# A graph and attention kernel: the edges' keys and degrees formed on GpSimd instead of VectorE

## The chip, the cores and the metric

The kernel runs on one core of one Trainium2 chip. The metric is device time in microseconds of one execution. A core has five engines that run side by side, each with a queue of its own: TensorE (PE, matrix products), VectorE (DVE), ScalarE (ACT), GpSimd (POOL) and SyncE (SP, which issues transfers). They meet through semaphores: an instruction adds to one when it is done, and another engine waits until it has reached a count.

## What is computed

The reference is a network of two layers over 3125 nodes with 256 features and 100,000 edges, sorted by destination. Each layer adds three things to x: a graph convolution over the edges, a linear attention, and a mixture of experts. What matters here is the first layer's graph part and attention, and the weights of the second layer's graph part:

```python
xn = _layernorm(x, axis=-1)
neigh = segment_sum(xn[src], dst, num_segments=n)      # layer 0, graph
h = (1.0 + eps) * xn + neigh
...
k = softmax(concat([mk, k], axis=-1), axis=-1)         # layer 0, attention
context = einsum('bhdn,bhen->bhde', k, v)
out = einsum('bhde,bhdn->bhen', context, softmax(q, axis=-2) * SCALE)
...
deg = segment_sum(ew2, dst2, num_segments=n_nodes)     # layer 1, graph
dinv = where(deg > 0, rsqrt(maximum(deg, 1e-30)), 0.0)
norm = dinv[src2] * ew2 * dinv[dst2]
```

The kernel doesn't gather rows edge by edge. It builds a dense matrix of edge counts and one of edge weights from one-hot matrices, and multiplies with them.

## The kernel before

**Edges in windows.** Destinations are cut into 1564 windows of two nodes each. Window number 128 g + p lies on partition p in group g, with 13 groups (`WG`) and so 13 x 128 = 1664 (`WN`) edge places on each partition. GpSimd's `windows_pool` gathers for every window 128 edges that start near its first one, 13 gathers of (dst, src, weight) triples into `H`. The views `edst`, `esrc` and `eew` are the three columns of these triples, so each steps over three words; `wrel` and `wlo` are written over `edst` and `esrc`.

**What VectorE does with them.** `places_dve` (13 instructions, `L323`) turns each destination into its place in the window: 0.5 or -0.5 in `wrel` for an edge of this window, anything else for a stranger. ScalarE squares that (`places_act`, `L334`), and `inside_dve` (`L338`) tests the square against 0.25 and counts the edges inside. `places_in_tiles_dve` splits the sender into a tile of 128 nodes (`L341`, a shift) and a place in it (`L343`, `wlo`). `tiles_dve` (`L347`) and `keys_dve` (`L351`) form the key from tile, place and test. TensorE turns `wlo` and the keys (`places_pe`, `keys_pe`), and ScalarE (`keys_act`) and VectorE (`keys16_dve`, `L404`) write them as bf16. `weights_dve` (`L310`, 26 instructions of 128 columns, each with a sum) forms the degree that each window gives to its two nodes, and signals `fold` 26 times; `degrees_pool` scales and stores it. `total_pe` and `good_dve` add the counts over the partitions and compare the sum with 100,000: where it differs, a slow path takes over.

**Attention around it.** `mix0_dve`, `mix0_act` and `mix0_pe` hold the order of work of this stage, written out by hand, and the edges' steps are set between those of the attention. In the loop over the seven groups j of tiles, TensorE turns the queries into a bank, ScalarE copies them to one of two buffers `qt`, TensorE multiplies with the context (`outs_pe`, `L816`), ScalarE takes squares and a root, and VectorE scales and adds to X (`L949` to `L959`). `keys_pe` stands behind the outputs of group 0 in TensorE's order. The buffers `qt` are the first two of the four 512-wide parts of `SC`:

```python
    qt = [SC[:, i, :] for i in range(2)]
    junk = [yob[0][:, 0, :], yob[0][:, 1, :], yob[1][:, 1, :], SC[:, 2, 0:D]]
```

**Behind it.** `count_pe`, `count_act` and `count_dve` run over 391 octets of windows in 25 blocks: VectorE makes one-hot matrices (`L1014` to `L1019`), TensorE multiplies them (`L1040` to `L1045`), and ScalarE brings the results out (`L1061`).

Of the kernel before, what the change touches and what calls it, by code (L numbers as in the profile page):

```python
# [20 lines left out]
EDGES = 100000  # L21
# [50 lines left out]
def program(nc, ctx, a, out):  # L72
# [96 lines left out]
    wprod = [wide_wb[:, i:i + 128] for i in range(2944, 2944 + 2 * WN, 128)]  # L169
# [3 lines left out]
    inside, goodc = pick[:, 65:66], pick[:, 66:67]  # L173
    deg2 = small[:, 970:970 + 2 * WG].rearrange("p (g r) -> p g r", r=2)
# [111 lines left out]
    def begins_dve(e, c):  # L286
        e.wait_ge(S("drow"), 16 * WG)
        for g in range(WG):
            c.add(e.tensor_scalar(rowf[:, g, :], rowi[:, g, :], w2h[:, g:g + 1], None, ALU.is_lt, ALU.add, accum_out=beg4[:, g:g + 1]))
        c.wait()  # L290
        c.add(e.scalar_tensor_tensor(beg4, row4, 128.0, beg4, ALU.mult, ALU.add))
        c.wait()
        e.tensor_copy(beg4i, beg4).then_inc(S("begins"), 1)

    def windows_pool(e):
        e.wait_ge(S("rows"), 1)
        for g in range(WG):
            e.indirect_dma_start(rowi[:, g, :], None, a["dst"].rearrange("(r k) -> r k", k=128),
                                 bass.IndirectOffsetOnAxis(ap=row4i[:, g:g + 1], axis=0)).then_inc(S("drow"), 16)
        e.wait_ge(S("begins"), 1)  # L300
# [6 lines left out]
    def weights_dve(e):  # L307
        for g in range(WG):
            for r in range(2):
                e.scalar_tensor_tensor(wprod[2 * g + r], wrel[:, g, :], r - 0.5, eew[:, g, :], ALU.is_equal, ALU.mult,  # L310
                                       accum_out=deg2[:, g, r:r + 1]).then_inc(S("fold"), 1)

    def degrees_pool(e):
        e.wait_ge(S("fold"), 2 * WG)
# [7 lines left out]
    def place_dve(e, g):  # L322
        return e.tensor_scalar(wrel[:, g, :], edst[:, g, :], w2h[:, g:g + 1], 1.0, ALU.subtract, ALU.subtract)  # L323

    def places_dve(e, c):
        e.wait_ge(S("edges"), 16 * WG)
        for g in range(WG - 1):
            c.add(place_dve(e, g))
        c.wait()
        place_dve(e, WG - 1).then_inc(S("mix0_dve"), 1)  # L330

    def places_act(e):
        e.wait_ge(S("mix0_dve"), M0V_REL + 1)
        e.activation(wok, wrel, ACT.Square).then_inc(S("mix0_act"), 1)  # L334

    def inside_dve(e):
        e.wait_ge(S("mix0_act"), M0A_PLACES + 1)
        e.tensor_scalar(wok, wok, 0.25, None, ALU.is_le, ALU.add, accum_out=inside).then_inc(S("inside"), 1)  # L338

    def places_in_tiles_dve(e, c):  # L340
        c.add(e.tensor_scalar(whii.bitcast(I32), esrc, 7, None, ALU.logical_shift_right))  # L341
        c.wait()
        e.scalar_tensor_tensor(wlo, whii.bitcast(I32), -128.0, esrc, ALU.mult, ALU.add).then_inc(S("wkey"), 1)  # L343

    def tiles_dve(e, c):
        e.wait_ge(S("wkey"), 1)
        c.add(e.scalar_tensor_tensor(whii, whii.bitcast(I32), 2.0, wrel, ALU.mult, ALU.add))  # L347

    def keys_dve(e, c):
        c.wait()  # L350
        e.scalar_tensor_tensor(wkey, whii, 1.5, wok, ALU.add, ALU.mult).then_inc(S("wkey"), 1)  # L351
# [22 lines left out]
    def places_pe(e):  # L374
        e.wait_ge(S("wkey"), 1)
# [3 lines left out]
    def keys_pe(e):  # L379
        e.wait_ge(S("wkey"), 2)  # L380
# [9 lines left out]
    def good_dve(e):  # L390
        e.wait_ge(S("total"), 1)
        e.tensor_scalar(goodc, B[3][:, 0:1], float(EDGES), None, ALU.is_equal).then_inc(S("good"), 1)
        e.tensor_scalar(flagi[0:1, 0:1], B[3][0:1, 0:1], float(EDGES), None, ALU.is_equal).then_inc(S("good"), 1)
# [261 lines left out]
    M0V_W, M0V_RS, M0V_GROW, M0V_REL, M0V_KMAX, M0V_DIAG, M0V_KSUB, M0V_MEM, M0V_MASKED, M0V_CTX, M0V_CWO = (  # L655
# [173 lines left out]
    def mix0_act(e):  # L829
# [71 lines left out]
    def mix0_dve(e, c):  # L901
        places_dve(e, c)
# [23 lines left out]
        inside_dve(e)  # L926
        q_norm_dve(e, c, 0)
        places_in_tiles_dve(e, c)
        good_dve(e)
# [14 lines left out]
        weights_dve(e)  # L944
# [259 lines left out]
    def count_act(e):  # L1204
        highs_act(e, 2)
        for b in range(T + 6):
            for i in range(8):
                if has_batch(b, i):
                    hots_act(e, 8 * b + i)
                if b == 0 and 1 <= i < 6:  # L1210
                    if i == 1:
                        e.wait_ge(S("fold"), 2 * WG)
# [113 lines left out]
    def degrees_dve(e, i, c):  # L1326
        if i == 4:
# [3 lines left out]
            e.tensor_scalar(dcol, dcol, 1.0, 1e-30, ALU.add, ALU.max).then_inc(S("degmax"), 1)  # L1331
        if i == 6:
            e.wait_ge(S("degroot"), 1)
# [4 lines left out]
    def degrees_act(e, i):  # L1338
        if i == 5:
            e.wait_ge(S("degmax"), 1)  # L1340
# [1362 lines left out]
```

## Time and profile before

| what | us |
|---|---|
| median of 3 runs (2229.63 to 2230.86) | 2230.41 |
| span of the profiled execution, first to last instruction | 2231.0 |
| its own time beside the span | not shown apart from it; the span lies 0.6 above the median of the runs |
| busy: PE 2089.4, DVE 1653.8, ACT 1233.5, POOL 566.9 | of 2231.0 |

A busy time says how long an engine was at work in all; it doesn't say in which stretch it held the others up. For that one reads the busy times of each stretch, and ahead of an instruction the idle time of its engine with what ended it.

### The profile page before, as it was taken

What the parts mean: (1) busy time and instruction counts of PE and PEld (TensorE: products, weight loads), DVE (VectorE), ACT (ScalarE), POOL (GpSimd) and SP (SyncE); (2) the same over time, 40 slices, a digit from 0 to 9 for tenths busy, and PEclk for the clock granted to TensorE, in tenths of its full rate; (3) what the DMA queues carried; (4) which work ended last, traced back from release to release, by engine and by line L of the source; (5) the groups of instructions that cost most, each with busy time, mean ns of one, the idle gap of its engine ahead of it and who ended that gap; (6) DMA issues with size and microseconds to landing.
All of it is one profiled execution on the core that took longest, in us unless ns stands there. A gap on an engine that the chain in (4) does not pass through costs nothing. (4 is left out here: it accounts for less than half of the span.)

```text
span 2231.0 us, 47270 instructions
## 1 busy us (share of the span) xinstructions
PE 2089.4 (94%) x18287; PEld 1958.7 (88%) x18287; DVE 1653.8 (74%) x3108; ACT 1233.5 (55%) x2876; POOL 566.9 (25%) x406
## 2 busy tenths in 40 slices
PE   5659999999879999998999999999999999999997
PEld 3549999999779999997788999999988999999996
DVE  6899888886578888884667666565667768888885
ACT  5656555555537677674543444444444336767664
POOL 3100000000036777761000000000000015777775
PEclk9879999999989999998999999999999999999998
DMA  4424343333448778775003666466641026777776
GB/s 123 145 65 115 96 114 90 99 111 104 161 158 234 236 218 241 227 222 144 1 26 89 189 188 182 122 182 195 189 145 47 25 93 184 239 231 222 240 215 171
DMA packets 241114, 339.04 MB, mean 152 GB/s; under 512 B 33407, under 2 KB 202546, under 8 KB 240754
## 3 DMA queue, kind: packets, MB, share of 16 engines
q1 hardware_dynamic: 208908, 296.19, 42.4%
q0 software_dynamic: 28528, 35.76, 8.6%
q10 hardware_dynamic: 3446, 3.97, 0.6%
q8 instruction: 150, 2.46, 0.5%
q14 instruction: 82, 0.67, 0.1%
HBM read 258.89 MB, written 76.95 MB: 151 GB/s over the span
## 5 line engine op out<-in xcount | busy, mean ns | idle before, releaser
L2011 POOL DMA_INDIRECT SC<-xd,slot_i x128 | 181.6, 1419 | 1423.8 <-DVE slot_q L1647 1291.6
L2436 PE MATMUL bank<-WB_r,XN_r 128*128 128x448 f32 x1400 | 398.7, 366 | 0.4 <-DVE X L2253 0.4
L2390 DVE TENSOR_TENSOR WB_r<-WB,WB_r 128x448 fp32r<-128x448 f32 x350 | 214.8, 624 | 169.1 <-ACT WB_r L2385 169.0
L2385 ACT CAST WB_r<-WB 128x448 fp32r<-128x448 f32 x350 | 198.2, 568 | 244.8 <-PE bank L2436 242.9
L2436 PEld LDWEIGHTS bank<-WB_r,XN_r 128*128 128x128 f32 x1400 | 262.4, 188 | 23.0 <-DVE X L2253 0.8
L1941 PE MATMUL bank<-SC_r,WB_r 128*128 128x256 f32 (+1 forms) x2064 | 250.8, 280 | 8.4 <-issue 6.3
L1941 PEld LDWEIGHTS bank<-SC_r,WB_r 128*128 128x128 f32 x2064 | 244.3, 188 | 12.6 <-issue 12.4
L1061 ACT CAST WB_r<-bank 128x200 fp32r<-128x200 f32 x391 | 145.3, 372 | 164.7 <-PE bank L1045 163.9
L1956 PE MATMUL bank<-R_r,H_r 128*128 128x256 f32 x1752 | 216.6, 283 | 5.0 <-DVE R_r L1852 5.0
L1956 PEld LDWEIGHTS bank<-R_r,H_r 128*128 128x128 f32 x1752 | 210.4, 190 | 5.4 <-issue 5.4
L1804 ACT ACTIVATE wb_<-bank,WB 128x256 f32<-128x256 f32 (+1 forms) x344 | 133.3, 477 | 79.7 <-PE bank L1941 40.6
L2017 POOL DMA_INDIRECT slot_p<-pd,slot_q x128 | 160.7, 1255 | 63.5 <-issue 35.7
L1941 PE MATMUL bank<-SC_r,XN_r 128*128 128x256 f32 x1392 | 169.5, 280 | 5.5 <-issue 4.9
L1941 PEld LDWEIGHTS bank<-SC_r,XN_r 128*128 128x128 f32 x1392 | 164.8, 188 | 9.5 <-issue 9.2
L1813 ACT ACTIVATE yo<-yo,slot_p 128x256 f32<-128x256 f32 x118 | 53.7, 502 | 209.0 <-DVE yo L1891 130.0
L1101 PE MATMUL bank<-H_r,WB_r 128*128 128x256 f32 x625 | 165.1, 300 | 0.0
L2436 PE MATMUL bank<-WB_r,R_r 128*128 128x448 f32 x448 | 164.5, 367 | 0.0
L1101 PE MATMUL bank<-XN_r,WB_r 128*128 128x256 f32 x625 | 154.0, 281 | 0.0
L1061 ACT COPY X<-bank 128x200 f32<-128x200 f32 x391 | 149.9, 383 | 0.0
L1015 DVE TENSOR_TENSOR SC<-R,DR 128x1024 bf16<-128x1024 bf16 x196 | 134.0, 684 | 0.0
L1101 PEld LDWEIGHTS bank<-XN_r,WB_r 128*128 128x128 f32 x625 | 119.3, 191 | 0.1
L1101 PEld LDWEIGHTS bank<-H_r,WB_r 128*128 128x128 f32 x625 | 119.0, 190 | 0.1
(462 smaller groups left out, 5139.1 us busy)
## 6 DMA issues: line engine op xcount, KB each, us to landing
WB<-adjw SPq DMA_DIRECT2D x350, 224.0 KB, 2.8
WB<-in_f_pack SPq DMA_DIRECT2D x127, 512.0 KB
WB<-in_f_pack SPq DMA_DIRECT2D x62, 640.0 KB
adjw<-X SPq DMA_DIRECT2D x24, 1600.0 KB, 7.6
WB<-in_f_pack SPq DMA_DIRECT2D x65, 516.0 KB
xd<-XN SPq DMA_DIRECT2D x15, 640.0 KB, 5.5
y<-X SPq DMA_DIRECT2D x10, 640.0 KB, 3.3
X<-y SPq DMA_DIRECT2D x6, 640.0 KB, 7.0
```

The source lines that it names most:

```text
L1015: e.tensor_tensor(by_two(hot_lo[s][:, 0:m, :]), row(iota16, o), along(lo2, o, 128), ALU.is_equal).then_inc(S("lo1"), 1)
L1061: e.copy(to[b % 2][:, :, 8 * j:8 * j + 8].rearrange("p h (q r) -> p q h r", r=2), bank[:, :, i]).then_inc(S(name), 1)
L1101: m = e.matmul(bk[:, 0:D], CNT[b % 2][:, h, :], x[:, h * D:(h + 1) * D], start=(h == 0 and x is xnh), stop=(h == T - 1 and x is xnl), skip ...
L1804: m = e.activation(st[:, q * w:(q + 1) * w], B[hp][:, q * TS:q * TS + w], gfun[L], bias=b[:, hc:hc + 1])
L1813: e.activation(ob[:, q, :], ob[:, q, :], ACT.Copy, scale=slot_p[:, 2 * i + q:2 * i + q + 1]).then_inc(S("obs"), 1)
L1941: m = e.matmul(B[hp][:, q * TS:q * TS + w], p[:, c * HID + hc * 128:c * HID + (hc + 1) * 128], x[:, c * w:(c + 1) * w], start=(c == 0 and ...
L1956: m = e.matmul(bk[:, s * D:(s + 1) * D], x[:, hc * w + s * 128:hc * w + (s + 1) * 128], p[:, hc * D:(hc + 1) * D], start=(hc == 0 and n == ...
L2011: e.indirect_dma_start(yin[i % 2][:, q * D:(q + 1) * D], None, XD, bass.IndirectOffsetOnAxis(ap=slot_i[:, 2 * i + q:2 * i + q + 1], axis=0 ...
L2017: e.indirect_dma_start(slot_p[:, 2 * i + q:2 * i + q + 1], None, PD.rearrange("(r k) -> r k", k=1), bass.IndirectOffsetOnAxis(ap=slot_q[:, ...
L2385: e.copy(split_w(m)[0], RAW[m % PR]).then_inc(S("whigh"), 1)
L2390: e.tensor_tensor(al, RAW[m % PR], ah.bitcast(F32), ALU.subtract).then_inc(S("wlow"), 1)
L2436: mm_ = e.matmul(conv_bank(k, band, c)[:, 0:PW], x[st][:, o], y, start=(st == 0 and i == 0), stop=(st == T - 1 and i == 2))
```

## The change

VectorE keeps one instruction for the edges, the shift (`tiles_dve`, now at the place of the placements and on all 1664 columns). Everything else moves to a new program of GpSimd, `edges_pool`, which runs behind its own gathers: the 13 placements, the sender's place, the key, the test, the counts and the degrees. VectorE's sums along a row, which were a by-product of an instruction, become additions of halves: 128 columns to 64, 32 and so on to 1, for all 13 groups at once (`sum_of_rows_pool`, seven instructions). Each step on GpSimd waits for the semaphore `edge` of the step before it. The count keeps its 13 groups apart (`kept`), and VectorE adds them behind the sum over the partitions. The products of the weights move from 26 pieces of `WB` to the first 1664 columns of `SC`, where the two buffers `qt` lie; ScalarE therefore waits for `fold` ahead of its first copy to `qt`.

```diff
-    wprod = [wide_wb[:, i:i + 128] for i in range(2944, 2944 + 2 * WN, 128)]
+    wprod = sc_all[:, 0:WN].rearrange("p (g n) -> p g n", g=WG)
...
-    def weights_dve(e):
+    PLACED, SCALED, SENDER, HALVED, TILED, KEPT, INSIDE, KEYED = (
+        WG, WG + 2, WG + 3, WG + 4, WG + 5, WG + 6, WG + 13, WG + 14)
+
+    def sum_of_rows_pool(e, of, to, n):
+        src, k = of, 64
+        while k:
+            dst = to if k == 1 else wprod[:, :, 0:k]
+            e.tensor_tensor(dst, src[:, :, 0:k], src[:, :, k:2 * k], ALU.add).then_inc(S("edge"), 1)
+            n += 1
+            e.wait_ge(S("edge"), n)
+            src, k = dst, k // 2
+        return n
+
+    def edges_pool(e):
+        e.wait_ge(S("edges"), 16 * WG)
         for g in range(WG):
-            for r in range(2):
-                e.scalar_tensor_tensor(wprod[2 * g + r], wrel[:, g, :], r - 0.5, eew[:, g, :], ALU.is_equal, ALU.mult,
-                                       accum_out=deg2[:, g, r:r + 1]).then_inc(S("fold"), 1)
+            e.tensor_scalar(wrel[:, g, :], edst[:, g, :], w2h[:, g:g + 1], 1.0, ALU.subtract, ALU.subtract).then_inc(S("edge"), 1)
+        e.wait_ge(S("mix0_dve"), M0V_TILE + 1)
+        e.tensor_scalar(wlo, esrc, 1.0, None, ALU.mult).then_inc(S("edge"), 1)
+        e.tensor_scalar(wprod, whii.bitcast(I32), -128.0, None, ALU.mult).then_inc(S("edge"), 1)
+        e.wait_ge(S("edge"), SCALED)
+        e.tensor_tensor(wlo, wlo, wprod, ALU.add).then_inc(S("edge"), 1)
+        e.tensor_scalar(whii, wprod, -1.0 / 64, 1.5, ALU.mult, ALU.add).then_inc(S("edge"), 1)
+        e.wait_ge(S("edge"), HALVED)
+        e.tensor_tensor(whii, whii, wrel, ALU.add).then_inc(S("edge"), 1)
+        e.wait_ge(S("mix0_act"), M0A_PLACES + 1)
+        e.tensor_scalar(wok_flat, wok_flat, 0.25, None, ALU.is_le).then_inc(S("edge"), 1)
+        e.wait_ge(S("edge"), KEPT)
+        sum_of_rows_pool(e, wok, kept.unsqueeze(2), KEPT)
+        e.tensor_tensor(wkey_flat, whii_flat, wok_flat, ALU.mult).then_inc(S("edge"), 1)
+        n = KEYED
+        for r in range(2):
+            e.wait_ge(S("edge"), n)
+            e.tensor_scalar(wprod, wrel, r - 0.5, None, ALU.is_equal).then_inc(S("edge"), 1)
+            e.wait_ge(S("edge"), n + 1)
+            e.tensor_tensor(wprod, wprod, eew, ALU.mult).then_inc(S("edge"), 1)
+            e.wait_ge(S("edge"), n + 2)
+            n = sum_of_rows_pool(e, wprod, deg2[:, :, r:r + 1], n + 2)
+        e.sem_inc(S("fold"), 2)
...
-    def places_dve(e, c):
+    def tiles_dve(e):
         e.wait_ge(S("edges"), 16 * WG)
-        for g in range(WG - 1):
-            c.add(place_dve(e, g))
-        c.wait()
-        place_dve(e, WG - 1).then_inc(S("mix0_dve"), 1)
+        e.tensor_scalar(whii.bitcast(I32), esrc, 7, None, ALU.logical_shift_right).then_inc(S("mix0_dve"), 1)
...
     def places_pe(e):
-        e.wait_ge(S("wkey"), 1)
+        e.wait_ge(S("edge"), SENDER)
...
     def keys_pe(e):
-        e.wait_ge(S("wkey"), 2)
+        e.wait_ge(S("edge"), KEYED)
...
     def total_pe(e):
         e.wait_ge(S("set"), 4)
-        e.wait_ge(S("inside"), 1)
-        e.matmul(B[3][:, 0:1], ones[:, :], inside, start=True, stop=True).then_inc(S("total"), 1)
+        e.wait_ge(S("edge"), INSIDE)
+        e.matmul(B[3][:, 0:WG], ones[:, :], kept, start=True, stop=True).then_inc(S("total"), 1)
...
+                if j == 0:
+                    e.wait_ge(S("fold"), 2)
                 if j >= 2:
                     e.wait_ge(S("ot"), 4 * (j - 1))
                 e.copy(qt[j % 2][:, 0:n], B[j % 2][:, 0:n]).then_inc(S("qt"), 1)
...
     def pool_program(e):
         windows_pool(e)
+        edges_pool(e)
         degrees_pool(e)
```

In `mix0_dve` the calls of the removed functions go, and in the rest of the diff semaphores get other names and counts (`begins` becomes a second count of `rows`, `degmax` a first one of `degroot`).

## Rows read from the trace of the kernel before

**Rows 1.** The page's totals: span, then busy us of each engine.

```profile
span 2231.0 us, 47270 instructions
PE 2089.4 (94%) x18287; PEld 1958.7 (88%) x18287; DVE 1653.8 (74%) x3108; ACT 1233.5 (55%) x2876; POOL 566.9 (25%) x406
```

**Rows 2.** Busy us (instructions) by stretch: PE, PEld, DVE, ACT, POOL, then clock, DMA.

```profile
104.00:120.00 16.00, 9.21 (x49) 7.74 (x49) 15.79 (x66) 7.91 (x23) 0.37 (x1) 0.89 0.00 0
...
146.00:182.00 36.00, 25.06 (x449) 24.24 (x450) 35.60 (x61) 23.39 (x69) 0.00 (x0) 0.72 0.22 66
182.00:300.00 118.00, 117.79 (x2018) 112.59 (x2015) 98.53 (x188) 67.12 (x262) 0.00 (x0) 1.00 0.40 113
```

**Rows 3.** Waits, 182 to 440 us: in total, times, longest.

```profile
DVE wb_ L1014 <- PE bank L1045: 43.4, 54, 1.2
```

**Rows 4.** VectorE in order of time: start us, us, what, count.

```profile
72.09 0.31 DVE L323 TENSOR_SCALAR H<-H,CB 128x128 f32<-128x128 int32 x1
...
72.31 2.80 DVE L323 TENSOR_SCALAR H<-H,CB 128x128 f32<-128x128 int32 x12
...
89.46 1.87 DVE L338 TENSOR_SCALAR_CACHE_REDUCE R<-R 128x1664 f32<-128x1664 f32 x1
...
94.91 1.34 DVE L341 TENSOR_SCALAR wide_wb<-H 128x1664 int32<-128x1664 int32 x1
96.28 2.46 DVE L343 SCALAR_TENSOR_TENSOR H<-wide_wb,H 128x1664 f32<-128x1664 int32 x1
...
99.25 2.45 DVE L347 SCALAR_TENSOR_TENSOR wide_wb<-wide_wb,H 128x1664 f32<-128x1664 int32 x1
...
101.81 1.89 DVE L351 SCALAR_TENSOR_TENSOR R<-wide_wb,R 128x1664 f32<-128x1664 f32 x1
...
108.92 3.85 DVE L404 TENSOR_SCALAR DR<-bank,small 128x1024 bf16<-128x1024 f32 x4
112.68 0.33 DVE L310 SCALAR_TENSOR_TENSOR wide_wb<-H 128x128 f32<-128x128 f32 x1
...
119.29 0.20 DVE L949 TENSOR_SCALAR small<-small 128x4 f32<-128x4 f32 x1
```

**Rows 5.** VectorE's groups by shape, 65 to 125 us: busy us, mean ns.

```profile
L878 DVE TENSOR_TENSOR wide_wb<-wide_wb,small 128x1408 f32<-128x1408 f32 x2 | 3.2, 1624 | 0.1
...
L922 DVE TENSOR_TENSOR wide_wb<-wide_wb,small 128x1408 f32<-128x1408 f32 x2 | 3.2, 1622 | 0.0
...
L878 DVE TENSOR_TENSOR wide_r<-wide_r,small 128x384 f32<-128x384 f32 x1 | 0.6, 558 | 0.0
...
L708 DVE TENSOR_SCALAR small<-small 128x25 f32<-128x25 f32 x1 | 0.2, 167 | 0.0
```

**Rows 6.** GpSimd in order of time: its last gather and its one arithmetic instruction.

```profile
61.96 0.94 POOL L302 DMA_INDIRECT H<-in_edges,small x1 [0.30 <-issue]
119.51 0.37 POOL L316 TENSOR_SCALAR small<-small 128x26 f32<-128x26 f32 x1 [56.61 <-DVE wide_wb L310]
```

**Rows 7.** DMA, 60 to 70 us in 40 slices: busy tenths of each.

```profile
DMA  7730966309384074663000000000000000000000
```

**Rows 8.** ScalarE in order of time: the squares, the first copy, the first root.

```profile
77.88 2.44 ACT L334 ACTIVATE R<-H 128x1664 f32<-128x1664 f32 x1
...
103.12 0.58 ACT L852 COPY SC<-bank 128x512 f32<-128x512 f32 x1 [0.61 <-PE bank L797]
...
110.41 0.20 ACT L863 ACTIVATE small<-small 128x4 f32<-128x4 f32 x1
```

**Rows 9.** The line of GpSimd's degree scaling: its queue's instructions, first and last start.

```profile
L316 POOLq MODIFY_POOL_CONFIG  x2: 42/42/43, 62.9 to 62.9; - x2
```

**Rows 10.** TensorE in order of time: the total, first outputs, key transposes.

```profile
91.48 0.35 PE L388 MATMUL bank<-small,ones 128*128 128x1 f32 x2
...
104.65 3.57 PE L816 MATMUL bank<-yo,SC 128*128 128x256 f32 x8
108.06 1.58 PE L371 MATMUL bank<-CB,R 128*128 128x128 f32 x13
```

More of the change, by code:

```diff
@@ L292, in begins_dve @@
         c.wait()
-        e.tensor_copy(beg4i, beg4).then_inc(S("begins"), 1)
+        e.tensor_copy(beg4i, beg4).then_inc(S("rows"), 1)
     def windows_pool(e):
@@ L299, in windows_pool @@
                                  bass.IndirectOffsetOnAxis(ap=row4i[:, g:g + 1], axis=0)).then_inc(S("drow"), 16)
-        e.wait_ge(S("begins"), 1)
+        e.wait_ge(S("rows"), 2)
         for g in range(WG):
@@ L313, in degrees_pool @@
     def degrees_pool(e):
-        e.wait_ge(S("fold"), 2 * WG)
+        e.wait_ge(S("fold"), 2)
         e.wait_ge(S("good"), 1)
@@ L318, in degrees_pool @@
         e.dma_start(DEG.rearrange("(g p r) -> p g r", g=WG, r=2), deg2).then_inc(S("deg_out"), 16)
[L322 to L325 removed]
+    def tiles_dve(e):
         e.wait_ge(S("edges"), 16 * WG)
[L327 to L330 removed]
+        e.tensor_scalar(whii.bitcast(I32), esrc, 7, None, ALU.logical_shift_right).then_inc(S("mix0_dve"), 1)
     def places_act(e):
[L333 removed]
+        e.wait_ge(S("edge"), PLACED)
         e.activation(wok, wrel, ACT.Square).then_inc(S("mix0_act"), 1)
[L336 to L345, printed above, removed]
[L346 to L351 removed]
     FILLS = 4
@@ L386, in total_pe, with good_dve @@
         e.wait_ge(S("set"), 4)
-        e.wait_ge(S("inside"), 1)
-        e.matmul(B[3][:, 0:1], ones[:, :], inside, start=True, stop=True).then_inc(S("total"), 1)
-    def good_dve(e):
+        e.wait_ge(S("edge"), INSIDE)
+        e.matmul(B[3][:, 0:WG], ones[:, :], kept, start=True, stop=True).then_inc(S("total"), 1)
+    def good_dve(e, c):
         e.wait_ge(S("total"), 1)
-        e.tensor_scalar(goodc, B[3][:, 0:1], float(EDGES), None, ALU.is_equal).then_inc(S("good"), 1)
-        e.tensor_scalar(flagi[0:1, 0:1], B[3][0:1, 0:1], float(EDGES), None, ALU.is_equal).then_inc(S("good"), 1)
+        c.add(e.tensor_reduce(inside, B[3][:, 0:WG], AX, ALU.add))
+        c.wait()
+        e.tensor_scalar(goodc, inside, float(EDGES), None, ALU.is_equal).then_inc(S("good"), 1)
+        e.tensor_scalar(flagi[0:1, 0:1], inside[0:1, :], float(EDGES), None, ALU.is_equal).then_inc(S("good"), 1)
     def keys_act(e):
@@ L849, in mix0_act @@
                 e.wait_ge(S("qT"), j + 1)
+                if j == 0:
+                    e.wait_ge(S("fold"), 2)
                 if j >= 2:
@@ L901, in mix0_dve @@
     def mix0_dve(e, c):
-        places_dve(e, c)
+        tiles_dve(e)
         q_sub_dve(e, c, 1)
@@ L1211, in count_act @@
                     if i == 1:
-                        e.wait_ge(S("fold"), 2 * WG)
+                        e.wait_ge(S("fold"), 2)
                     e.copy(xnh[:, fifth(i - 1)], xn_all[:, fifth(i - 1)]).then_inc(S("xnh"), 1)
@@ L1330, in degrees_dve @@
             c.wait()
-            e.tensor_scalar(dcol, dcol, 1.0, 1e-30, ALU.add, ALU.max).then_inc(S("degmax"), 1)
+            e.tensor_scalar(dcol, dcol, 1.0, 1e-30, ALU.add, ALU.max).then_inc(S("degroot"), 1)
         if i == 6:
-            e.wait_ge(S("degroot"), 1)
+            e.wait_ge(S("degroot"), 2)
             c.add(e.reciprocal(dcol, dcol))
```

15 lines of the change are left out of this document (6 added, 9 removed).

## The prediction

> **What bounds the kernel now.** I read the page's totals first, then the busy time by stage, the waits of the long stage, and last the rows of each engine around the change. The totals name TensorE, 2089.4 of 2231.0 us [rows 1], but that is an average over stages with different limits. By stages [rows 2]: from 104 to 120 us VectorE works 15.79 of 16 us, from 146 to 182 it works 35.60 of 36, and TensorE about 60 to 70% in both. From 182 us TensorE works 117.79 of 118 and VectorE waits for it: 43.4 us in 54 waits up to 440 us [rows 3]. So the edges' preparation and the attention loop behind it belong to VectorE, and TensorE's long run starts when VectorE has fed it. Neither stage waits for a transfer, so whatever moves the attention loop (`L949` and below, first row at 119.29 us [rows 4]) moves the end by as much.
>
> **What comes off VectorE.** Rows 4 hold the pieces: 13 placements (0.31 and 2.80, nearly back to back, 2.9 together), the count `L338` 1.87, the remainder `L343` 2.46, the keys `L347` and `L351` 2.45 and 1.89, and 26 degree passes from 112.68 to 119.29, 6.6. That is 18.2 us. The shift `L341`, 1.34, is only moved to the place of the placements. Added is one reduction over 13 columns of a bank and its wait; the small VectorE row of [rows 5], 0.17, bounds it, and nothing bounds it at 1 us or more. If nothing else held the loop, VectorE would reach it at about 119.3 - 18.0 = 101.3 us, a gain of 18 us. This is the gain that the change is after; the question is what GpSimd costs.
>
> **What GpSimd gets.** Its gathers were issued by 62.9 us [rows 6] and the transfers had ended by about 64.8 [rows 7]: of 40 slices of 0.25 us the last busy one is the 19th. Then it was idle until 119.5. Thirteen placements fit there: at VectorE's 0.31 us they take 4 us, at 2.2 times that (below) 8.9, so they end between 69 and 74 us. ScalarE's squares need them at 77.88 [rows 8], so they are covered, and they would cost only if they took over 1 us each. Two configuration instructions stand in GpSimd's queue at 62.9 [rows 9]; whatever they start was hidden behind that idle time and now has 8.6 us of it left, so I price it at nothing, at most the few microseconds by which it passes 73.4. At 73.4 (72.09 + 1.34) VectorE's shift is ready and the serial chain of GpSimd begins. Each step waits for the one before it:
>
> - six passes over 128x1664 with one input (sender to float, tile times -128, the affine step, the test for 0.25, twice the test for the row);
> - four with two inputs, one of them strided in the edges' tile (low part, key, two products with the weights), and the key times its test, contiguous;
> - three sums by halves, seven additions each, 1651 elements.
>
> The trace shows no such pass on GpSimd, so I price it from both sides. VectorE's prices are the lower side: one input 1.34 (`L341`), strided two inputs 2.45 (`L347`), contiguous 1.89 (`L351`) [rows 4]. For the additions, the 1408- and 384-wide rows give (1624 - 558)/1024 = 1.04 ns an element and 0.16 us fixed [rows 5], so a sum costs 7 x 0.16 + 1651 x 0.00104 = 2.8. Together 6 x 1.34 + 4 x 2.45 + 1.89 + 3 x 2.83 = 28.2 us. The chain would then end at F = 73.4 + 28.2 = 101.6. The other side is GpSimd's one arithmetic row, 0.37 us for 128x26 [rows 6]. Read as a rate it is 14 ns an element, which would put F hundreds of microseconds later; read against VectorE's 0.167 us for 128x25 of the same kind of instruction, a tensor with a scalar [rows 5], it says that GpSimd takes 2.2 times as long. I take the ratio: it is the one pair of rows in which both engines do the same thing at nearly the same size, though both are mostly fixed cost. Then the chain is 28.2 x 2.22 = 62.6 us and F = 136.
>
> The Trainium skill, GPSIMD Engine Reference, section Performance versus the Vector engine, says that a GpSimd addition of two float tensors takes 1.96 times VectorE's time, while one-input work is near line rate; it also advises against moving elementwise work there. The 2.2 of the row agrees in direction. By the page's figure on the two-input passes alone the sum would be 8.0 + 1.96 x 20.2 = 47.6, F = 121 and the time about 2241.
>
> **The wait that this makes.** The products now live in the first 1664 columns of `SC`, which also holds the two `qt` buffers. So ScalarE's first copy to `qt` waits for `fold`, the end of the whole GpSimd chain, degrees included. That copy ran at 103.12 [rows 8]. Behind it on ScalarE stand every copy, square and root of the loop; TensorE's first output matmuls wait for it, and its key transposes stand behind those matmuls; VectorE's `L404` waits for the transposes. From F on: the copy 0.58 [rows 8], then 108.06 - 104.65 = 3.4 from the first output matmul to the key transposes [rows 10], 108.92 - 108.06 = 0.9 to VectorE's first `L404`, and 3.8 for the four of them (108.92 to 112.68 [rows 4]). The loop starts at F + 8.6. ScalarE's first root is ready sooner: it ended 110.61 - 104.65 = 6.0 after the first output matmul, so at F + 6.6. From there on the loop is VectorE's as before. Shift of the end = F + 8.6 - 119.3 = F - 110.7. With F = 136 that is +25.3.
>
> TensorE's total also waits on GpSimd, for the count's sum: 4 x 1.34 + 2 x 2.45 + 2.83 = 13.1, times 2.22 is 29, at 102.5 instead of 91.48 [rows 10], and the context matmuls stand behind it. VectorE's short steps after the context follow 11 us later too, near 111, and its last normalizations near 116. All of that ends before F and costs nothing while F is above some 116; at VectorE's pace the total isn't late at all (86.5).
>
> **Sum.** The profiled execution spans 2231.0, and the median of the runs is 2230.41, so I add to either alike: 2230.4 + 25.3 = 2256.
>
> **Rivals.**
> 1. *GpSimd keeps VectorE's pace.* F = 101.6, the shift is -9.1, time 2221. The break-even is F = 110.7, that is 37.3/28.2 = 1.32 times VectorE's price; under 1.16 the gain passes 0.2% (4.5 us, about what a measurement of this kernel can tell from no change), over 1.48 the loss does. For it: most passes are long, so the fixed part that fills the small row matters less. Against it: that row, and some 30 waits between dependent instructions, which VectorE's prices don't hold.
> 2. *Only two-input passes are dear.* One-input passes at 1.34, the rest at 2.22 times: 8.0 + 44.8 = 52.8, F = 126.2, +15.5, time 2246.
> 3. *The two engines block each other.* VectorE still runs passes with two inputs from the same memory while GpSimd's chain runs: one query shift at 1.62, the key shifts 3.24 [rows 5], two normalizing products of the first form's size, 3.24, and two of 384 columns, 1.1: 9 us. If GpSimd waits these out, F = 145, time 2265; what VectorE loses is covered by its idle time before F. No row here shows both engines at such work together, since GpSimd idled. The Trainium skill, SBUF — State Buffer, section Who interferes with whom, states this rule: a VectorE instruction with two inputs in SBUF and a reading GpSimd instruction exclude each other for their whole length. No row here bears on it.
>
> **How the numbers follow.** Pace near 2.2, with little blocking (2250 to 2262): 45 in 100, the forecast. Rival 2 and paces between 1.5 and 2 (2235 to 2250): 20. Rival 3, or a pace above 2.4 (over 2262): 18. Break-even within 4.5 us (2226 to 2235): 9. Faster: 8. The likeliest time is 2256. The range runs from 2232 (all below it about 14 in 100) to 2276 (some 5 above). So faster 0.08, same 0.09, slower 0.83.
>
> **What the changed profile would show.** Right: GpSimd busy from about 65 us to past 130 with 46 arithmetic instructions; its 1664-wide two-input passes at 4 to 5.5 us and one-input ones near 3; ScalarE's first `qt` copy released by GpSimd; VectorE idle ahead of its key passes and its loop 25 us later than 119.3; the stages behind it as long as before. Wrong: a two-input pass near 2 us with the `qt` copy before 105 (rival 1); one-input passes near 1.4 (rival 2); passes of one shape whose lengths differ by whole VectorE instructions (rival 3); or a later stage that gives some of the shift back, which I price at nothing because TensorE has 0.2 us of slack in 118 there.

## The result and the profile after

The changed kernel takes 2270.92 us (median of 4 runs, 2267.26 to 2274.22), the kernel before 2230.64 beside it (2229.63 to 2232.93). The ratio is 1.0174, with an interval from 1.0162 to 1.0186; times 2230.6 that is 38.8 us more, where 25.3 were forecast. 2270.9 lies inside the range, but above the forecast's own band (2250 to 2262): it is in the band that the prediction gave to rival 3 or to a slower pace (over 2262). The profiled execution, whose rows stand here, took 2267.26 with a span of 2265.8, 3.7 below the median; the reading below goes by the stage of the change.

The page's totals, as in [rows 1]:

```profile
span 2265.8 us, 47249 instructions
...
PE 2086.8 (92%) x18287; PEld 1956.7 (86%) x18287; DVE 1656.2 (73%) x3039; ACT 1233.5 (54%) x2876; POOL 647.7 (29%) x451
```

Some 18 us of work left VectorE, and yet its busy time is 2.4 us longer than in [rows 1]. GpSimd in order of time says what it was given (start, us, engine, line, count; in brackets the idle time before and what ended it):

```profile
65.81 13.65 POOL L326 TENSOR_SCALAR H<-H,CB 128x128 f32<-128x128 int32 x13 [2.58 <-DMA H<-in_edges,small]
79.38 6.00 POOL L328 TENSOR_SCALAR H<-H 128x1664 f32<-128x1664 int32 x1
...
94.04 1.77 POOL L332 TENSOR_SCALAR wide_wb<-SC 128x1664 f32<-128x1664 f32 x1
95.89 5.34 POOL L334 TENSOR_TENSOR wide_wb<-wide_wb,H 128x1664 f32<-128x1664 f32 x1
101.18 5.81 POOL L336 TENSOR_SCALAR R<-R 128x1664 f32<-128x1664 f32 x1
...
127.01 6.39 POOL L317 TENSOR_TENSOR SC<-SC 128x832 f32<-128x832 f32 x6
...
143.21 4.92 POOL L317 TENSOR_TENSOR SC<-SC 128x832 f32<-128x832 f32 x6
148.20 0.21 POOL L317 TENSOR_TENSOR small<-SC 128x13 f32<-128x13 f32 x1
```

The placements hold GpSimd until 79.4, the serial chain runs from there without a gap, and its last addition ends at F = 148.41 (forecast: 136). VectorE beside it, in the same view:

```profile
68.05 1.62 DVE L896 TENSOR_TENSOR wide_wb<-wide_wb,small 128x1408 f32<-128x1408 f32 x1
...
72.56 1.30 DVE L361 TENSOR_SCALAR wide_wb<-H 128x1664 int32<-128x1664 int32 x1
...
75.42 1.77 DVE L896 TENSOR_TENSOR wide_wb<-wide_wb,small 128x1408 f32<-128x1408 f32 x1
...
79.86 4.25 DVE L917 TENSOR_TENSOR small<-small 128x128 f32<-128x128 f32 x1
...
84.67 0.29 DVE L917 TENSOR_TENSOR small<-small 128x128 f32<-128x128 f32 x1
...
90.40 3.96 DVE L896 TENSOR_TENSOR wide_r<-wide_r,small 128x384 f32<-128x384 f32 x1
...
94.60 8.11 DVE L940 TENSOR_TENSOR wide_wb<-wide_wb,small 128x1408 f32<-128x1408 f32 x2
```

`L917` shows it best: the same instruction twice, 4.25 and 0.29 us. `L896` on 384 columns takes 3.96 where [rows 5] has 0.56; the two of `L940` take 8.11 where [rows 5] has 3.2 (`L922`). Ten rows between 75 and 131 us are stretched in this way, by 20.6 us in all. That is waiting that the trace books as busy; 20.6 less the 18.2 taken away is the 2.4 by which VectorE's total rose.

GpSimd waits for VectorE as well. Ten of its 13 placements take about 0.85 us, one starting 0.77 after the other; three take more. Read one by one:

```profile
68.15 2.25 POOL L326 TENSOR_SCALAR H<-H,CB 128x128 f32<-128x128 int32 x1
...
72.65 1.95 POOL L326 TENSOR_SCALAR H<-H,CB 128x128 f32<-128x128 int32 x1
...
76.05 1.86 POOL L326 TENSOR_SCALAR H<-H,CB 128x128 f32<-128x128 int32 x1
```

Each of the three starts while one of the first three VectorE instructions above (68.05, 72.56, 75.42) is running, and ends 0.7 us behind it. Together they lose 3.5 us.

Then the wait. ScalarE's first copies to `qt`, TensorE's outputs and key transposes, VectorE's first `keys16_dve` and its loop:

```profile
148.55 1.07 ACT L870 COPY SC<-bank 128x512 f32<-128x512 f32 x2 [22.39 <-POOLq L348]
```

```profile
149.19 3.53 PE L832 MATMUL bank<-yo,SC 128*128 128x256 f32 x8 [22.56 <-ACT SC L870]
152.55 1.58 PE L385 MATMUL bank<-CB,R 128*128 128x128 f32 x13
```

```profile
153.26 3.85 DVE L420 TENSOR_SCALAR DR<-bank,small 128x1024 bf16<-128x1024 f32 x4 [21.49 <-PE bank L385]
157.03 0.16 DVE L962 TENSOR_SCALAR small<-small 128x4 f32<-128x4 f32 x1
```

All three engines stood idle for about 22 us, and the first copy was released by GpSimd's queue at the end of the chain (`L348` signals `fold`). The loop starts at 157.03, 37.7 after the 119.29 of [rows 4]. The wait itself, and then the two long stages of [rows 2], cut 37.74 us later:

```profile
120.00:148.00 28.00, 6.07 (x45) 5.04 (x44) 7.02 (x10) 2.95 (x4) 26.65 (x17) 0.65 0.00 0
...
183.74:219.74 36.00, 25.10 (x454) 24.19 (x455) 35.72 (x61) 23.32 (x69) 0.00 (x0) 0.73 0.22 66
219.74:337.74 118.00, 117.79 (x2018) 112.60 (x2016) 98.49 (x189) 67.28 (x263) 0.00 (x0) 1.00 0.40 113
```

From 120 to 148 the core waits for GpSimd. From 219.7 TensorE is full, 117.79 of 118, as it was from 182 before. Its first one-hot product comes at 179.09 (before: 141.38), its last 37.6 later than before. So the loop's start sets the end of the counting. Behind it this one execution gives some of the shift back: it is still 37.5 where TensorE's `L1954` begins (693.0 us) and 33.4 where its `L2360` begins (1183.9), and the spans differ by 34.8 (2265.8 against 2231.0). The medians differ by 38.8, so not every execution does so; what the later stages add or take is a few us and isn't explained here.

### The profile page after: what moved, and what is told of

The parts are those of the page before. It is cut to its first block and busy times, and to the rows that moved or that the text cites. A ratio compares the mean times of both kernels' runs of the same rounds, so it can differ in the third digit from the quotient of the medians.

```text
span 2265.8 us, 47249 instructions
## 1 busy us (share of the span) xinstructions
PE 2086.8 (92%) x18287; PEld 1956.7 (86%) x18287; DVE 1656.2 (73%) x3039; ACT 1233.5 (54%) x2876; POOL 647.7 (29%) x451
## 5 line engine op out<-in xcount | busy, mean ns | idle before, releaser
L2024 POOL DMA_INDIRECT SC<-xd,slot_i x128 | 190.6, 1489 | 1437.2 <-DVE slot_q L1660 1298.6
L1954 PE MATMUL bank<-SC_r,WB_r 128*128 128x256 f32 (+1 forms) x2064 | 250.7, 280 | 9.1 <-issue 7.1
L1954 PEld LDWEIGHTS bank<-SC_r,WB_r 128*128 128x128 f32 x2064 | 244.1, 188 | 13.5 <-issue 13.4
L1954 PE MATMUL bank<-SC_r,XN_r 128*128 128x256 f32 x1392 | 168.9, 280 | 5.9 <-issue 5.1
L1954 PEld LDWEIGHTS bank<-SC_r,XN_r 128*128 128x128 f32 x1392 | 164.2, 188 | 10.0 <-issue 9.5
L2030 POOL DMA_INDIRECT slot_p<-pd,slot_q x128 | 152.1, 1189 | 64.0 <-issue 33.8
L1826 ACT ACTIVATE yo<-yo,slot_p 128x256 f32<-128x256 f32 x118 | 53.7, 502 | 208.5 <-DVE yo L1904 154.2
```

What stands on the lines that cost most here:

```text
L1826: e.activation(ob[:, q, :], ob[:, q, :], ACT.Copy, scale=slot_p[:, 2 * i + q:2 * i + q + 1]).then_inc(S("obs"), 1)
L1954: m = e.matmul(B[hp][:, q * TS:q * TS + w], p[:, c * HID + hc * 128:c * HID + (hc + 1) * 128], x[:, c * w:(c + 1) * w], start=(c == 0 and ...
L2024: e.indirect_dma_start(yin[i % 2][:, q * D:(q + 1) * D], None, XD, bass.IndirectOffsetOnAxis(ap=slot_i[:, 2 * i + q:2 * i + q + 1], axis=0 ...
L2030: e.indirect_dma_start(slot_p[:, 2 * i + q:2 * i + q + 1], None, PD.rearrange("(r k) -> r k", k=1), bass.IndirectOffsetOnAxis(ap=slot_q[:, ...
```

## Experiments

The gap to the forecast is 12.4 us in F. Three questions: what the wait for `fold` costs, what GpSimd's passes cost by themselves and what the engines take from each other, and whether any of this work is worth moving. "First one-hot" below is the start of TensorE's first `count_pe` product; before it is at 141.38. Times of one run each are called so.

### 1. The degrees elsewhere

The products move out of the `qt` buffers to a free stretch of `WB`, behind the context; the copy waits for the count only.

```diff
+    wdeg = wide_wb[:, 3200:3200 + WN].rearrange("p (g n) -> p g n", g=WG)
...
+        e.wait_ge(S("mix0_pe"), M0P_CTX + 1)
...
-            e.tensor_scalar(wprod, wrel, r - 0.5, None, ALU.is_equal).then_inc(S("edge"), 1)
+            e.tensor_scalar(wdeg, wrel, r - 0.5, None, ALU.is_equal).then_inc(S("edge"), 1)
...
-                    e.wait_ge(S("fold"), 2)
+                    e.wait_ge(S("edge"), INSIDE)
```

> The products and halves of the degrees go to 1664 columns of the keys' dead area instead of SC, behind the context matmuls; ScalarE's first qt copy waits only for the count's sum (113.6 us in the changed kernel), not for the degrees. Theory 1, the wait for the whole chain sets the loop: the loop starts when VectorE's last normalization (131.8) and its four key passes (3.85) are done, near 136 instead of 157, and the time falls by some 21 us to about 2250. Rival, the blocking between VectorE and GpSimd sets the time: the degree passes, 31 us of them, then block the loop's own instructions, and the time stays above 2262.

Measured: 2254.88, ratio 1.0093 (1.0077 to 1.011). The loop starts at 138.58, 18.4 earlier than after, but the first one-hot product comes at 163.87, only 15.2 earlier. VectorE between them:

```profile
131.31 3.59 DVE L909 TENSOR_TENSOR wide_r<-wide_r,small 128x384 f32<-128x384 f32 x1
134.82 3.84 DVE L422 TENSOR_SCALAR DR<-bank,small 128x1024 bf16<-128x1024 f32 x4
138.58 0.15 DVE L964 TENSOR_SCALAR small<-small 128x4 f32<-128x4 f32 x1
...
145.12 0.27 DVE L964 TENSOR_SCALAR small<-small 128x4 f32<-128x4 f32 x1 [2.25 <-ACT small L883]
```

A blocked normalization (3.59 for 0.57) now lies on the path. Then the loop stalls 2.25 us for ScalarE's root, which waits for TensorE's outputs: TensorE had stood idle 7.46 us before the transposes at 138.63, and its second block of outputs took 3.59 us (`L834`, 140.38) where the same block after the change took 1.89. The windows, this kernel's and then the changed kernel's at the same step of the loop:

```profile
138.50:144.50 6.00, 5.87 (x23) 5.05 (x24) 4.22 (x10) 2.86 (x9) 5.53 (x6) 0.56 0.00 0
```

```profile
157.00:163.00 6.00, 5.92 (x36) 5.25 (x36) 5.75 (x15) 5.15 (x14) 0.00 (x0) 1.00 0.01 1
```

The granted clock was 0.56, most of it at the lower of the two levels (1.2 GHz), against 1.00 (2.4 GHz). Without the wait for `fold` the first one-hot product is 15.2 us earlier of the 37.7, and by the ratios the kernel 18.0 us faster of the 38.8. The rest stays: in this kernel the loop waits for the context, and that for GpSimd's count.

### 2. VectorE held still

VectorE waits behind its shift until GpSimd is done, so GpSimd's chain runs alone.

```diff
         tiles_dve(e)
+        e.wait_ge(S("fold"), 2)
         q_sub_dve(e, c, 1)
```

> VectorE waits behind its shift until GpSimd's whole chain is done, so neither can block the other. Theory 1, part of the chain is blocking: from the end of the placements to the end of the degrees it takes about 57 us instead of 69.0, with the test for 0.25 near 1.8 instead of 5.8 and the tile product near 1.8 instead of 4.4. Rival, the passes are that long by themselves (a test is dear, an integer input is dear): about 69 us again, the test near 5.8. The time as a whole is longer than 2271 in either case, since VectorE's work then follows the chain.

Measured (one run, 2292.32): the chain takes 63.1 us, from 78.19 to 141.32, between the two theories; in the changed kernel it took 69.0. So blocking costs GpSimd's chain 5.9 us, not 12. And VectorE's two normalizing products take 3.16 together. GpSimd's rows are the clean prices, the last five placements first:

```profile
74.36 3.91 POOL L326 TENSOR_SCALAR H<-H,CB 128x128 f32<-128x128 int32 x5
...
78.19 5.94 POOL L328 TENSOR_SCALAR H<-H 128x1664 f32<-128x1664 int32 x1
84.06 4.39 POOL L329 TENSOR_SCALAR SC<-wide_wb 128x1664 f32<-128x1664 int32 x1
88.54 4.17 POOL L331 TENSOR_TENSOR H<-H,SC 128x1664 f32<-128x1664 f32 x1
92.79 1.58 POOL L332 TENSOR_SCALAR wide_wb<-SC 128x1664 f32<-128x1664 f32 x1
...
98.47 4.41 POOL L336 TENSOR_SCALAR R<-R 128x1664 f32<-128x1664 f32 x1
...
108.25 3.69 POOL L339 TENSOR_TENSOR R<-wide_wb,R 128x1664 f32<-128x1664 f32 x1
112.03 5.15 POOL L343 TENSOR_SCALAR SC<-H 128x1664 f32<-128x1664 f32 x1
...
121.39 4.91 POOL L317 TENSOR_TENSOR SC<-SC 128x832 f32<-128x832 f32 x6
```

The passes with one input are the dearest, one excepted: `L332`, a product and an addition in one instruction, takes 1.58. The placements settle too: VectorE stands still from 73.7, and the five placements behind 74.36 don't wait: 0.78 us each, strided integers and all. The two long ones of this run (2.34 and 1.96, at 67.89 and 72.47) lie beside VectorE's instructions again.

### 3. The placements back on VectorE

```diff
     def tiles_dve(e):
         e.wait_ge(S("edges"), 16 * WG)
+        for g in range(WG):
+            e.tensor_scalar(wrel[:, g, :], edst[:, g, :], w2h[:, g:g + 1], 1.0, ALU.subtract, ALU.subtract).then_inc(S("edge"), 1)
```

> VectorE keeps the 13 placements as well (2.9 us at 72.6), GpSimd begins with the sender's pass. Theory 1, the late end of GpSimd's placements (79.4 instead of 73.9) passes into the end one for one: the chain begins near 76.9 and ends 2.5 us earlier, the loop starts near 154.5, the time is about 2268. Rival, GpSimd only meets other VectorE instructions and loses the lead again: the chain ends at 148 or later.

Measured (one run): 2267.73, near the 2268 expected, but the changed kernel itself ran from 2267.26 to 2274.22, so the time of one run tells little here. F falls by 3.45 to 144.96 and the loop starts at 154.25, but the first one-hot product comes only 1.2 us earlier: TensorE's key transposes took 2.60 us instead of 1.58, and in the first 6 us of the loop (154.2 to 160.2) its mean granted clock was 0.72, between the two levels, against 1.00 in the changed kernel (157 to 163):

```profile
154.20:160.20 6.00, 5.90 (x27) 5.32 (x28) 4.38 (x12) 3.65 (x12) 0.00 (x0) 0.72 0.00 0
```

That the clock was lower is shown; why it was here, after an idle time of 23.65 us that is close to the 22.56 of the changed kernel, stays open.

### 4. Only the degrees on GpSimd, beside the kernel before

All else is left on VectorE; the products go to the place of experiment 1, behind the context and the last normalization.

```diff
-    wprod = [wide_wb[:, i:i + 128] for i in range(2944, 2944 + 2 * WN, 128)]
+    wdeg = wide_wb[:, 3200:3200 + WN].rearrange("p (g n) -> p g n", g=WG)
...
+    def weights_pool(e):
+        e.wait_ge(S("mix0_pe"), M0P_CTX + 1)
+        e.wait_ge(S("qn"), 3)
...
-        weights_dve(e)
```

> The kernel before with one part of the change: only the degrees go to GpSimd, in the keys' dead area, behind the last normalization (109 us), in 31 us that nothing waits for until the second block of the counting. Theory 1, what counts is the wait and the engine's pace where somebody waits: VectorE's loop starts 6.6 us sooner, at 112.7, and the time falls by 3 to 6.6 us to 2224 to 2228. Rival, blocking: GpSimd's passes hold up the loop's small instructions on VectorE and the one-hot products, and the time is 2231 or more.

Measured: 2234.06, ratio 1.0000 (0.9991 to 1.0009). The rival is right. VectorE enters its loop 6.1 us earlier, and gives it all back inside:

```profile
113.16 1.73 DVE L966 TENSOR_SCALAR small<-small 128x4 f32<-128x4 f32 x1
...
126.88 2.67 DVE L461 TENSOR_TENSOR WB<-WB 128x512 f32<-128x512 f32 x1
...
133.25 1.64 DVE L461 TENSOR_TENSOR H<-H,R 128x512 f32<-128x512 f32 x1
134.82 1.92 DVE L966 TENSOR_SCALAR small<-small 128x4 f32<-128x4 f32 x1
```

```profile
109.67 5.19 POOL L324 TENSOR_SCALAR wide_wb<-H 128x1664 f32<-128x1664 f32 x1 [46.55 <-DVE wide_r L907]
```

An instruction on 128x4 (0.16 by itself) takes 1.73 and ends at 114.9, when GpSimd's test ends (109.67 + 5.19 = 114.86). The stretched rows add up to 6.5 us; the first one-hot product comes at 141.80, 0.4 later than before.

### 5. The degrees left out

Experiment 4 without the sums: both degrees of every window are set to one. The second layer's values and its routing differ with that (the last gathers number 56 instead of 60), so its total of 2207.27 (ratio 0.9890, 0.9875 to 0.9906) can't be set beside the others, and only the stretch up to the counting is read.

```diff
-        n = 0
-        for r in range(2):
...
+        e.memset(deg2, 1.0).then_inc(S("edge"), 1)
+        e.wait_ge(S("edge"), 1)
```

> The kernel with only the degrees on GpSimd, but with GpSimd's passes left out: GpSimd sets the degrees to one and signals at once, so this kernel leaves out the degrees' sums. Theory 1, VectorE's loop is worth its time one for one and GpSimd's passes ate the gain by blocking: without them the loop starts near 112.7, no instruction in it is stretched, and the time is about 2234 less 6.6, some 2227. Rival, something else holds the loop (ScalarE, TensorE at its lower clock): the loop starts sooner and then waits, and the time stays at 2232 or more.

Measured: the loop starts at 112.86, no row in it is stretched (`L959` 0.16 and 0.17, `L454` 0.85), one wait of 1.25 for ScalarE's root appears, and the first one-hot product comes at 136.3, 5.1 earlier than before. That is what the degrees cost this stretch while VectorE does them. At the same point experiment 4 is 5.5 us later, and the two kernels differ by GpSimd's passes alone: they took the gain back.

### 6. The same in thirds

The tests and the products of experiment 4 are cut in three, by groups.

```diff
+    THIRDS = (slice(0, 4), slice(4, 8), slice(8, WG))
...
+            for o in THIRDS:
+                e.tensor_scalar(wdeg[:, o, :], wrel[:, o, :], r - 0.5, None, ALU.is_equal).then_inc(S("edge"), 1)
```

> As the kernel with only the degrees on GpSimd, with each test and each product cut in three (four, four and five of the 13 groups), so that GpSimd's longest instruction is near 2.1 us instead of 5.2. If blocking lasts until the other engine's instruction ends, VectorE's stretched instructions lose about 3 us less, and the time is 0.1 to 0.2% under the kernel before, 2229 to 2232. If blocking doesn't depend on the other's length, no difference: 2234.

Measured: 2229.23, ratio 0.9986 (0.9976 to 0.9995), first one-hot at 140.30. GpSimd ends no earlier than in experiment 4 (141.4 against 140.0), but the 128x4 instruction now waits 1.3 us at most.

### 7. Prices of single passes

Experiment 2 with eight scratch passes in the chain, each with one property changed (operation, type, stride, width).

```diff
+        e.tensor_scalar(wprod, whii, 1.0, None, ALU.mult).then_inc(S("edge"), 1)
...
+        e.tensor_scalar(wprod, whii, 0.25, None, ALU.is_le).then_inc(S("edge"), 1)
...
+        e.tensor_scalar(wprod, eew, 1.0, None, ALU.mult).then_inc(S("edge"), 1)
...
+        e.tensor_scalar(wprod, wint, 1.0, None, ALU.mult).then_inc(S("edge"), 1)
...
+        e.tensor_scalar(wprod, whii, 0.25, None, ALU.max).then_inc(S("edge"), 1)
...
+        e.tensor_scalar(wprod[:, 0, :], whii[:, 0, :], w2h[:, 0:1], 1.0, ALU.subtract, ALU.subtract).then_inc(S("edge"), 1)
```

> The kernel with VectorE held, and eight more passes of GpSimd into its scratch ahead of the degrees, each alone on the machine: a product of a contiguous float tensor (expected 1.6 us for 1664 columns), a test (4.4), a product of the strided weights, a product of a contiguous integer view (4.4), a maximum, and three 128-wide placements from contiguous float, contiguous integer and strided float. If stride is what is dear, the strided float product takes over 4; if test and integer are dear by themselves, it takes under 3, the maximum is near 1.6, and the placements differ by the input's type. The time is some 20 us over the held kernel.

Measured (one run; its total, 2315.89, holds the scratch passes):

```profile
111.49 4.41 POOL L343 TENSOR_SCALAR SC<-wide_wb 128x1664 f32<-128x1664 f32 x1
115.99 4.41 POOL L345 TENSOR_SCALAR SC<-wide_wb 128x1664 f32<-128x1664 f32 x1
120.48 5.15 POOL L347 TENSOR_SCALAR SC<-H 128x1664 f32<-128x1664 f32 x1
125.71 4.41 POOL L349 TENSOR_SCALAR SC<-wide_wb 128x1664 f32<-128x1664 int32 x1
...
134.69 0.73 POOL L353 TENSOR_SCALAR SC<-wide_wb,CB 128x128 f32<-128x128 f32 x1
```

A product, a test and an integer input all cost 4.41, the maximum 4.40, where 1.6 was expected of the product and the maximum; the stride of three words adds 0.74. I read this as: what made `L332` cheap is neither its operation nor its type but its form with two operations (experiment 8 narrows that). A placement costs 0.73 here, 0.72 from integers and 0.78 from strided floats; the changed kernel's 13 took 1.05 each on average because three of them waited.

### 8. Two operations in every pass

```diff
-        e.tensor_scalar(wlo, esrc, 1.0, None, ALU.mult).then_inc(S("edge"), 1)
-        e.tensor_scalar(wprod, whii.bitcast(I32), -128.0, None, ALU.mult).then_inc(S("edge"), 1)
+        e.tensor_scalar(wlo, esrc, 1.0, 0.0, ALU.mult, ALU.add).then_inc(S("edge"), 1)
+        e.tensor_scalar(wprod, whii.bitcast(I32), -128.0, 0.0, ALU.mult, ALU.add).then_inc(S("edge"), 1)
...
-            e.tensor_scalar(wprod, wrel, r - 0.5, None, ALU.is_equal).then_inc(S("edge"), 1)
+            e.tensor_scalar(wprod, wrel, r - 0.5, 1.0, ALU.is_equal, ALU.mult).then_inc(S("edge"), 1)
```

> The changed kernel, with a second, empty operation (add zero or times one) in its five one-input passes that had a single one. With GpSimd alone every one-input pass of a single operation took 4.4 us from a contiguous tensor, whatever the operation and the input's type, and the one with two operations 1.6. If the single-operation form is what is dear, these passes fall to 1.6 to 2.5 us, the chain ends near 133 instead of 148.4, ScalarE's copy and the loop follow one for one, and the time is about 2256. Rival, the affine pass was short for another reason: the passes stay at 4.4 to 6 and the time at 2271.

Measured: 2267.66, ratio 1.0156 (1.0141 to 1.0172); my theory was half right.

```profile
78.89 2.40 POOL L328 TENSOR_SCALAR H<-H 128x1664 f32<-128x1664 int32 x1
81.25 1.61 POOL L329 TENSOR_SCALAR SC<-wide_wb 128x1664 f32<-128x1664 int32 x1
...
129.89 6.54 POOL L343 TENSOR_SCALAR SC<-H 128x1664 f32<-128x1664 f32 x1 [0.17 <-POOL small L317]
```

Product and addition fall to 2.40 and 1.61; a test and a product rise to 5.83 from a contiguous tensor and to 6.54 from a strided one. Among the forms tried, only product with addition is fast. The 5.83 shows the other side as well:

```profile
92.96 5.94 DVE L933 TENSOR_SCALAR rows<-rows 128x256 f32<-128x256 f32 x1
```

This VectorE instruction took 0.28 in experiment 2; it started 0.04 behind GpSimd's test (92.92 to 98.75) and ended 0.15 behind it.

### 9 to 11. The same edit on experiments 1, 4 and 6

```diff
-            e.tensor_scalar(wdeg, wrel, r - 0.5, None, ALU.is_equal).then_inc(S("edge"), 1)
+            e.tensor_scalar(wdeg, wrel, r - 0.5, 1.0, ALU.is_equal, ALU.mult).then_inc(S("edge"), 1)
```

> The same in the kernel whose degrees lie outside SC. If the count's sum is what the loop then waits for, through the total, the context matmuls and the normalizations, it comes 10 us sooner, the loop starts near 128 instead of 138.6, and the time is about 2244 instead of 2255; still over the kernel before, whose loop starts at 119.3. Rival, blocking moves with the passes and the loop starts at 135 or later: 2252.

> Only the degrees on GpSimd, with the two tests in the form with two operations: 5.2 us each becomes about 2, GpSimd's work 24 us instead of 30. Blocking in proportion to GpSimd's work: VectorE loses about 5 us instead of 6.5, and the time is 2 us or so under the version with 5.2 us tests, about 0.999 of the kernel before. If a stretched instruction waits only in the longest passes, it gains more, 0.998.

> Both remedies: tests with two operations, tests and products in thirds. If the shorter instructions of GpSimd are what helped, 0.997 to 0.998 of the kernel before, 2225 to 2228. If cutting further only adds starts, the same as in thirds alone, 0.9986.

Measured: on experiment 1 2250.67, ratio 1.0079 (1.0064 to 1.0095): the loop starts at 132.96, 5.6 earlier, between the two expectations and close to the 6.5 us by which the count's sum came sooner (107.46 against 113.96), so there the loop does follow the count. On experiments 4 and 6 the edit touches only the tests, and these became longer, so both came out above what was expected: 2235.99, 1.0010 (1.0001 to 1.0019), and 2232.14, 0.9999 (0.9989 to 1.0008). That failure is useful: the same work in a longer instruction, with nothing else changed (below).

### 12. Degrees without tests

One product (weight times the flag of the inside edges), its sum, the product times the place, its sum, and half the first sum minus and plus the second; long passes in thirds. The key gets a place of its own so that the flag stays, and ScalarE's counting program waits for the first three products.

```diff
+        for o in THIRDS:
+            e.tensor_tensor(wdeg[:, o, :], eew[:, o, :], wok[:, o, :], ALU.mult).then_inc(S("edge"), 1)
...
+        n = sum_of_rows_pool(e, wdeg, first, 3, whalf)
+        for o in THIRDS:
+            e.tensor_tensor(wdeg[:, o, :], wdeg[:, o, :], wrel[:, o, :], ALU.mult).then_inc(S("edge"), 1)
```

> Only the degrees on GpSimd, and without a test in them: the weight times VectorE's inside flag, its sum by halves, the same times the place (0.5 or -0.5), its sum, and from both sums the two degrees. The keys go to the keys' dead area so that the flags stay. Products in thirds; GpSimd's work falls from 30 to about 20 us and its longest instruction to 2 us. If what VectorE loses goes with the length of GpSimd's instructions and with how long GpSimd is busy in the loop, the gain of 6.6 us is kept but for some 2 us: 0.998 of the kernel before, 2226 to 2229, and faster than the version in thirds with tests (0.9986). If it goes by the number of GpSimd's instructions, no better than 0.9986.

Measured: 2228.52 against 2233.25, ratio 0.9977 (0.9968 to 0.9986): faster than both kernels. GpSimd is done at 130.7, 9 us earlier than in experiment 4, VectorE's small instructions wait at most 0.83, and the first one-hot product comes at 138.29.

The five forms of "degrees alone" in one table. "Longest" is GpSimd's longest single instruction beside the loop; "loop" is the time from VectorE's entry into it to the first one-hot product (22.1 in the kernel before, 23.4 in experiment 5, where GpSimd does nothing beside it). Both come from one profiled execution each:

| form | longest, us | loop, us | first one-hot against 141.38 | ratio |
|---|---|---|---|---|
| 10: whole passes, slow test | 6.59 | 31.4 | +3.7 | 1.0010 (1.0001 to 1.0019) |
| 4: whole passes | 5.24 | 28.6 | +0.4 | 1.0000 (0.9991 to 1.0009) |
| 11: thirds, slow test | 2.68 | 29.1 | +1.3 | 0.9999 (0.9989 to 1.0008) |
| 6: thirds | 2.16 | 27.6 | -1.1 | 0.9986 (0.9976 to 0.9995) |
| 12: thirds, no test | 1.95 | 25.2 | -3.1 | 0.9977 (0.9968 to 0.9986) |

With the same test, the loop is shorter in thirds than in whole passes (10 and 11, 4 and 6); cut alike, it is shorter with the faster test (10 and 4, 11 and 6). So the length of one instruction isn't all: experiment 11 has shorter ones than experiment 4 and a longer loop, with GpSimd at work for 34 us instead of 30. The intervals of the ratios overlap between neighbours in the table; 12 stands clear of 4, 10 and 11.

## Why the prediction was right and where not

**What bounds the kernel: right.** The loop's start moved by 37.7 and the end by 38.8 (36.1 to 41.5); the stages up to the end of the counting kept their lengths.

**The wait for `fold` and what follows it: right to the tenth.** Loop at F + 8.6 was worked out; 157.03 - 148.41 = 8.62. So the error is all in F: 148.4 for 136, in three terms. The total of 2270.9 falls into the range, but not by the sum that was worked out: what was priced at nothing makes most of the gap.

1. *The placements: 6.0 us past the 73.4 of the shift, the step that was wrong.* "Covered, and they would cost only if they took over 1 us each": that bound was drawn at ScalarE's squares (77.88), but GpSimd's own next step stood ready at 73.4, where 0.66 us each was the limit and the 0.68 priced was already over it. Measured: they began at 65.8 instead of 64.8 (1.0 us), would have taken 10.1 us at the pace of the ten that did not wait, where 8.6 fitted (1.5), and lost 3.5 us behind three VectorE instructions. VectorE's 0.31 times 2.2 was only a little cheap (0.77 from start to start); the rest is blocking.
2. *The chain by itself: 63.1 for 62.6, right by errors that cancel.* The six one-input passes cost 26.6 where 17.9 were priced (+8.7), the four strided two-input ones 16.3 for 21.8, the key 3.69 for 4.2, the three sums 15.6 for 18.8. That the ratio of one pair of small rows came out for the sum is luck; it is a poor price for any one pass.
3. *Blocking: 5.9 us on GpSimd's chain and 3.5 on its placements, priced at nothing in the forecast.* Rival 3 named it and priced it at 9; measured are 9.4, though two of the three waits of the placements are for instructions that rival 3 doesn't list. The sign that it gave is there too: the same six additions take 6.39 us beside VectorE and 4.92 once it stands idle. The mechanism is shown, by experiment 2 on GpSimd's side and by experiments 4, 5, 8, 10 and 12 on VectorE's. The Trainium skill, SBUF — State Buffer, section Who interferes with whom, is borne out in the main: two-input VectorE instructions wait out GpSimd's (8.11 us for 3.16); it also lists scalar instructions among those that can, in a mode with two ports, and the 128x4 one that took 1.73 agrees, though no run here shows the mode. Not every overlap costs, as the trace has it: in experiment 11 the 128x4 instruction took 0.15 at 113.61, inside a GpSimd test that ran from 112.28 to 114.44, and a two-input one took its usual 0.85 at 132.58, inside a later one (131.41 to 134.10). Why these two didn't wait stays open. That "what VectorE loses is covered by its idle time" held for the changed kernel (20.6 us of stretching, all ended by 131.8); it doesn't hold where VectorE sets the pace, which is why experiment 4 gained nothing.

**Rival 1** (VectorE's pace) is out: every two-input pass took 1.7 to 2 times VectorE's 2.45 and 1.89. **Rival 2** was the wrong way round: 4.41 against VectorE's 1.34 with one input, 3.69 against 1.89 with two. The Trainium skill, GPSIMD Engine Reference, section Performance versus the Vector engine, gives 1.96 for an addition of two inputs; the trace has 1.95 for a contiguous product (3.69 against 1.89). One-input work at roughly line rate, which the same page states in its section Engine selection and by which the time was 2241, fits only product with addition (1.58 against VectorE's 1.34).

**The count: later than said, and harmless.** TensorE's total came at 113.70 (forecast 102.5) and VectorE's last normalization ended at 131.8 (116), still ahead of F. Experiments 1 and 9 show that it is the next bound: with the wait for `fold` gone, 20.8 us of the loss remain.

**Left open:** which overlaps of the two engines cost a wait and which don't, the cause of the lower clock in experiment 3, and what makes the later stages differ by a few us from run to run.

## What to carry to other kernels

Work moved off a busy engine has to be priced twice: what it costs on the other engine, by rows of the same instruction form, and what the two engines' instructions cost each other while both run. A task that fits an idle time has to be held against the next step of its own engine as well as against the engine that reads its result. Look at which buffer the moved work writes: putting scratch where the next stage begins turned a side job into the thing that everybody waits for, at 15 to 18 us. If work must go to GpSimd beside a VectorE that sets the pace, cut it in short instructions and leave out the expensive forms; here that turned no gain (1.0000) into 0.9977, of which the last step also left out some of GpSimd's work.

## What the runs showed of the hardware

- GpSimd's one-input pass over 1664 contiguous columns costs 4.41 us for a product, a test or an integer input alike, 1.58 to 1.61 for a product with an addition, and 5.83 for a test with a product (6.5 where strided).
- A VectorE instruction of 0.16 us on 128x4 took 3.13 us in experiment 10, until GpSimd's instruction ended, and one of 0.28 us on 128x256 took 5.94 in experiment 8. It goes both ways: a GpSimd placement of 0.85 us took up to 2.25 beside a VectorE instruction of 1.62. Such waits stand in the trace as busy time, without a releaser; one finds them by comparing rows of the same shape, one by one where the view merges them.
- TensorE's clock in a stretch that begins after an idle time differed between nearly equal kernels (0.56, 0.72 and 1.00 over the first 6 us of the loop in experiments 1 and 3 and the changed kernel), and the two kernels with the lower clock lost 3.2 and 1.6 us of their earlier start inside the loop.
